# Softmax attention: the score maxima from the high halves alone, four heads at once on quarters of the array, in four banks, with one transpose of the maxima

## The reference

```python
q = x @ w_q + b_q                      # x is layernorm(x); 16 heads of 32 columns
k = context @ w_k + b_k
v = context @ w_v + b_v
scores = einsum('bqhd,bkhd->bhqk', q, k) * (1 / sqrt(32))
weights = softmax(scores, axis=-1)
out = einsum('bhqk,bkhd->bqhd', weights, v) @ w_o + b_o
```

## Time and profile before

| | us |
|---|---|
| median of 3 runs (1720.33 to 1724.28) | 1723.47 |
| the profiled execution | 1720.95 |
| its span | 1718.7 |
| softmax attention, first maximum to last output | about 648 to 1430 |
| one batch of it, in the middle | 94.35 |

### The profile page before, as it was taken

How to read it: one execution, slowest core, us unless ns; L and a number is a source line. 1 busy time by engine, 2 the same in 40 slices (tenths; PEclk the granted TensorE clock), 3 DMA queues, 4 the chain that set the end, 5 groups by cost and what they waited for, 6 DMA issues and landing times. The chain is left out here.

```text
span 1718.7 us, 29488 instructions
## 1 busy us (share of the span) xinstructions
PE 1586.6 (92%) x8932; PEld 719.5 (42%) x8932; DVE 1227.2 (71%) x1756; ACT 1138.3 (66%) x1895; POOL 1023.1 (60%) x738
## 2 busy tenths in 40 slices
PE   5999878998999977999999999999999988999998
PEld 3545433444444432334444444444444423444443
DVE  4978898997989745676676767676767766655553
ACT  5667599787888734665657666665657567556662
POOL 4777436666677723565657666675756665545452
PEclk9989999999999997999999999999999989999999
DMA  8410000000000112121211212121201110010001
GB/s 309 149 70 36 1 1 1 1 1 1 0 1 1 62 48 76 32 58 26 58 34 36 57 26 57 28 55 30 59 24 40 40 44 25 25 43 30 24 24 50
DMA packets 60463, 72.22 MB, mean 42 GB/s; under 512 B 14416, under 2 KB 40016, under 8 KB 59856
## 3 DMA queue, kind: packets, MB, share of 16 engines
q1 hardware_dynamic: 56944, 62.22, 12.3%
q10 hardware_dynamic: 3424, 8.91, 1.3%
HBM read 37.40 MB, written 8.39 MB: 27 GB/s over the span
## 5 line engine op out<-in xcount | busy, mean ns | idle before, releaser
L1556 DVE TENSOR_REDUCE s_mx<-bank 128x1 f32<-128x512 f32 x512 | 336.8, 684 | 198.5 <-PE bank L1684 192.5
L1443 ACT ACTIVATE s_E<-bank 128x512 f32<-128x512 f32 x512 | 293.7, 595 | 198.7 <-PE bank L1698 173.4
L1342 POOL TENSOR_TENSOR s_E<-s_E 128x1024 f32<-128x1024 f32 x128 | 300.5, 2367 | 122.0 <-PE bank L1706 114.5
L1684 PE MATMUL bank<-s_KA,s_QA 96*128 96x512 f16 x512 | 193.2, 388 | 17.3 <-DMA s_KA<-sm_cx 7.9
L1698 PE MATMUL bank<-s_QA,s_KA 97*128 97x512 f16 x512 | 195.7, 384 | 3.3 <-DMA s_QA<-s_mrow 1.1
L1335 POOL TENSOR_TENSOR sm_cx<-s_qkf,sm_cx 128x512 f16<-128x512 f32 x64 | 76.4, 1194 | 175.9 <-ACT sm_cx L1421 175.7
L1867 POOL TENSOR_TENSOR sm_cx<-m_xf,sm_cx 128x512 f16<-128x512 f32 x60 | 84.1, 1407 | 105.7 <-ACT sm_cx L1909 105.7
L1706 PE MATMUL bank<-s_E,s_V 128*32 128x512 f32 x1024 | 136.5, 605 | 4.3 <-ACT s_E L1443 4.3
L1075 PE MATMUL bank<-sm_zz,w1raw 128*128 128x512 f16 x256 | 99.4, 388 | 30.7 <-DVE sm_cx L962 15.5
L1098 PE MATMUL bank<-f_w2q,w2raw 128*128 128x512 f16 x512 | 121.8, 379 | 0.6 <-DVE w2raw L950 0.3
L772 POOL TENSOR_TENSOR sm_wkv<-sm_wkv,sm_cx 128x511 f32<-128x511 f32 x48 | 66.1, 1378 | 92.5 <-DVE sm_wkv L962 83.0
(11 more groups left out here) (264 smaller groups left out, 4078.6 us busy)
## 6 DMA issues: line engine op xcount, KB each, us to landing
sm_cx<-in_ctx SPq DMA_DIRECT2D x16, 768.0 KB, 4.5
s_QA<-sm_cx SPq DMA_DIRECT2D x384, 32.0 KB, 1.9
s_KA<-sm_cx SPq DMA_DIRECT2D x372, 32.0 KB, 1.9
X<-in_x SPq DMA_DIRECT2D x8, 1024.0 KB, 6.9
out_x<-X SPq DMA_DIRECT2D x8, 1024.0 KB, 4.3
w1raw<-in_w ACTq DMA_DIRECT2D x1, 4096.0 KB, 14.6
w2raw<-in_w ACTq DMA_DIRECT2D x1, 4096.0 KB, 28.2
w1raw<-in_wq SPq DMA_DIRECT2D x1, 1024.0 KB, 5.4
```

The source lines that it names most:

```text
L1342: e.tensor_tensor(into, into, other, ALU.add).then_inc(s_sum.sem, 1)
L1443: e.activation(E[:, SLOT[k] + h, :], SC[u % 2][:, :], ACT.Exp, scale=1.0 / float(np.sqrt(DH)))\
L1556: e.tensor_reduce(mx[:, q, h:h + 1], MX[q % 2][:, :], AX.X, ALU.max).then_inc(s_red.sem, 1)
L1684: e.matmul(MX[k % 2][:, :], QA[0:MROW, m, h, q * P:(q + 1) * P], KA[0:MROW, m, h, :], start=True, stop=True).then_inc(s_mx.sem, 1)
```

## The change

It does five things.

1. **Maxima from the high halves.** `maxima` multiplies the high half of the queries (32 rows of one head) by the high half of the keys, without stacking. Head h sits on partitions 32h to 32h + 31 of qkh, so four matmuls, one a head, use four row quarters of the array. Each writes a whole bank of its own: head h goes to bank h. A query tile of a group is one such **quad**; four quads a step instead of 16 full matmuls.
2. **The banks.** The quads write banks 0 to 3, that is, the two score banks too. The PSUM tensors become pairs of banks, so that one `tensor_reduce` reads two banks (128 x 2 x 512 to 128 x 2): two of them a quad, 8 a step instead of 16.
3. **Four phases a step.** At the start of each tile (u = 0, 4, 8, 12) TensorE waits for all exponentials so far, makes the quad for the next group, then the `attend` of the tile before (and at u = 0 and u = 8 one half of the denominators), and then waits for the first reduction (banks 0 and 1) before the tile's first score.
4. **One transpose.** mx is laid out so that a single transpose gives 16 x 128 in bank 2; mrow is 16 x 128, and the DMA spreads it. `rows` (transpose, copy and DMA) moves from the end of the step before to the start of the group's own step. The quad at u = 0 also waits for the copy (same bank).
5. **The rest of the order.** New tables; the work between two scores stands in `between(u)`. ScalarE's numerators and the division (`late`, now two steps after the group) move to the start of a step, ahead of the first exponential; `divided(b, 0)` to the end of step 2. GpSimd's second half of the sums moves to the start of the next step. qkh is double-buffered. Before the loop, the first group's maxima no longer wait for the stacking DMAs.

The diff, cut to what the prediction speaks of:

```diff
-        banks = [ctx.enter_context(nc.psum_tensor(f"bank{i}", [P, 512], F32)) for i in range(8)]
+        pairs = [ctx.enter_context(nc.psum_tensor(f"bank{i}", [P, 2, 512], F32)) for i in range(4)]
+        banks = [pairs[i // 2][:, i % 2, :] for i in range(8)]
...
+    Q_AT = ((-1, -1, 1, 3), (-1, -1, -1, -1), (0, 1, 2, 3), (-1, -1, 1, 3))
+    K_AT = ((3, 5, 7), (0, 1, 2), (7, 9, 11), (3, 5, 7))
+    V_AT = ((9, 11, 11, 13), (4, 6, 7, 7), (14, 15, 15, 15), (9, 11, 11, 13))
+    T_AT = (10, 12, 13, 15)
+    O_AT = ({}, {3: ((0, 0), (0, 1)), 5: ((0, 2),), 7: ((0, 3),), 8: ((1, 0),), 9: ((1, 1),), 11: ((1, 2), (1, 3)),
+                 13: ((2, 0),), 14: ((2, 1),), 15: ((2, 2), (2, 3))},
+            {5: ((3, 0),), 7: ((3, 1),), 11: ((3, 2),), 13: ((3, 3),)}, {})
+    RES_AT = ({}, {8: 0, 12: 1}, {-1: 2, 14: 3}, {})
+    STATS_AT, MOMENTS_AT, NORM_AT = {0: (0, 1), 4: (2, 3)}, 4, (0, 1, 2, 3)
...
-        SC, MX, NUM, DEN, R6, R7 = banks[0:2], banks[2:4], banks[4], banks[5], banks[6], banks[7]
+        SC, MX, MAXED, NUM, DEN, R6, R7 = banks[0:2], banks[0:4], pairs[0:2], banks[4], banks[5], banks[6], banks[7]
...
-        qkh, qkl = rows_of(cx, 4 * KC, 4 * KC + 2), rows_of(cx, 4 * KC + 2, 4 * KC + 4)
+        qkh = (rows_of(cx, 4 * KC, 4 * KC + 2), sb("qkh", [P, 2, S], F16))
...
@@ GpSimd, step @@
+                if m == 3:
+                    divided(b, 0)
+                if div:
+                    summed(*div, 1, 0)
+                    summed(*div, 1, 1)
+                if m == 2 and not last:
+                    context(b + 1)
+                if late and m != 2:
+                    divided(*late)
                 if proj:
-                    if m == 2:
-                        context(b + 1)
                     low(*proj, 0)
...
@@ ScalarE, rows and step @@
-                e.activation(mrow[:, :], MX[0][0:4, :], ACT.Copy, scale=-1.0 / MS).then_inc(s_mrow.sem, 1)
+                e.activation(mrow[:, :], MX[2][0:4 * TT, 0:P], ACT.Copy, scale=-1.0 / MS).then_inc(s_mrow.sem, 1)
-                e.dma_start(QA[MROW:MROW + 1, m, :, :], mrow[0:4, :]).then_inc(s_md[m].sem, 16)
+                e.dma_start(QA[MROW:MROW + 1, m, :, :].rearrange("o h (q n) -> o (h q) n", n=P), mrow[:, :]).then_inc(s_md[m].sem, 16)
...
+                rows(b, m)
+                if first and m == 0:
+                    e.wait_ge(s_lo, 2)
+                    e.wait_ge(s_raw[3], 32)
+                if div:
+                    numerators(*div)
+                if m == 1:
+                    queries(*proj, 0)
                 if m == 2 and not last:
                     for c in range(KC):
                         context(b + 1, c)
-                if proj:
-                    queries(*proj, 0)
-                if div and N_UNIT[m] < 0:
-                    numerators(*div)
+                if late and m != 2:
+                    divided(*late)
+                if m == 3 and not last:
+                    values(b + 1, 0)
                 for u in range(UNITS):
-                    if u == UNITS - 1 and nxt:
-                        rows(*nxt)
-                    if m == 1 and u - 1 in T_UNITS:
+                    exponential(b, m, u)
+                    if m == 1 and u in T_AT:
                         if last:
-                            shifted(T_UNITS.index(u - 1))
+                            shifted(T_AT.index(u))
                         else:
-                            high(b + 1, T_UNITS.index(u - 1), R7)
-                    exponential(b, m, u)
+                            high(b + 1, T_AT.index(u), R7)
                     if last and m == 3 and u in MIX_UNITS:
                         mix(MIX_UNITS.index(u))
-                    if div and u == N_UNIT[m]:
-                        numerators(*div)
-                    if proj and u == K_UNITS[m][-1] + 1:
+                    if proj and u == 3 and m != 1:
+                        queries(*proj, 0)
+                    if proj and u == (7, 3, 11, 7)[m]:
                         queries(*proj, 1)
-                    if proj and u == min(V_UNITS[m][-1] + 1, UNITS - 1):
+                    if proj and u == (13, 7, None, 13)[m]:
                         values(*proj)
-                    if m == 2 and u == A_LATE:
+                    if m == 2 and u == UNITS - 1:
                         divided(b, 0)
-                    if div and m != 1 and u == A_UNIT:
-                        divided(*div)
+                if last and m == 3:
+                    divided(b, 2)
...
@@ VectorE @@
-            def maximum(b, m, k):
-                h, q = divmod(k, TT)
+            def maxima(b, m, q):
                 s_mT.wait(e, b, m)
-                s_mx.wait(e, b, 16 * m + k + 1)
-                e.tensor_reduce(mx[:, q, h:h + 1], MX[q % 2][:, :], AX.X, ALU.max).then_inc(s_red.sem, 1)
+                s_mx.wait(e, b, TT * m + q + 1)
+                for i in range(2):
+                    e.tensor_reduce(mx[:, 2 * i:2 * i + 2, q], MAXED[i][:, :, :], AX.X, ALU.max).then_inc(s_red.sem, 1)
...
@@ TensorE @@
-            def maximum(b, m, k):
-                h, q = divmod(k, TT)
-                if k == 0:
-                    e.wait_ge(s_sh[m][0].sem, s_sh[m][0].count(b, NSH))
-                    e.wait_ge(s_sh[m][1].sem, s_sh[m][1].count(b, NSH))
+            def maxima(b, m, q):
+                if q == 0:
+                    e.wait_ge(s_qkh.sem, s_qkh.count(b, 2 * m + 2))
                     s_mrow.wait(e, b, m)
-                s_red.wait(e, b, 16 * m + k - 1)
-                e.matmul(MX[k % 2][:, :], QA[0:MROW, m, h, q * P:(q + 1) * P], KA[0:MROW, m, h, :],
-                         start=True, stop=True).then_inc(s_mx.sem, 1)
+                s_red.wait(e, b, 2 * (TT * m + q))
+                high = qkh[m % 2]
+                for h in range(4):
+                    head = slice(h * DH, (h + 1) * DH)
+                    last = e.matmul(MX[h][:, :], high[head, 0, q * P:(q + 1) * P], high[head, 1, :], start=True, stop=True)
+                last.then_inc(s_mx.sem, 1)
 
             def rows(b, m):
-                e.wait_ge(s_red.sem, s_red.count(b, 16 * (m + 1)))
-                for q in range(TT):
-                    last = e.transpose(MX[0][0:4, q * P:(q + 1) * P], mx[:, q, :], ident[:, :])
-                last.then_inc(s_mT.sem, 1)
-
-            def score(b, m, u):
+                e.wait_ge(s_red.sem, s_red.count(b, 2 * TT * (m + 1)))
+                e.transpose(MX[2][0:4 * TT, 0:P], mx[:, :, :].rearrange("p h q -> p (h q)"), ident[:, :]).then_inc(s_mT.sem, 1)
+
+            def score(b, m, u, nxt):
                 t, h = divmod(u, 4)
                 if u == 0:
+                    for w in range(2):
+                        e.wait_ge(s_sh[m][w].sem, s_sh[m][w].count(b, NSH))
                     e.wait_ge(s_md[m].sem, s_md[m].count(b, 1))
+                if nxt and h == 0:
+                    e.wait_ge(s_red.sem, s_red.count(nxt[0], 2 * (TT * nxt[1] + t) + 1))
...
+                def between(u):
+                    if m == 1 and u in T_AT:
+                        transposed(b + 1, T_AT.index(u), last)
+                    if proj:
+                        for c in range(KD):
+                            if Q_AT[m][c] == u and (u >= 0 or c):
+                                queries(*proj, 0, c)
+                        for c in range(KC):
+                            if K_AT[m][c] == u:
+                                queries(*proj, 1, c)
+                    if not first:
...
+                if proj and Q_AT[m][0] < 0:
+                    queries(*proj, 0, 0)
+                rows(b, m)
+                if first and m == 0:
+                    s_V.wait(e, 0, 2)
+                    e.wait_ge(s_lo, 2)
+                between(-1)
+                for u in range(UNITS):
+                    t, h = divmod(u, 4)
+                    if nxt and h == 0:
+                        if t == 0:
+                            s_mrow.wait(e, b, m + 1)
+                        e.wait_ge(s_ex.sem, s_ex.count(b, 16 * m + 4 * t))
+                        maxima(*nxt, t)
+                    if t and h == 0:
+                        attend(b, m, t - 1)
+                    if div and u == 0:
+                        attend(*div, TT - 1)
+                        denominators(*div, 0)
+                    if div and u == 4 * DN_TILE:
+                        denominators(*div, 1)
+                    score(b, m, u, nxt)
+                    between(u)
...
```

155 lines of the change are left out of this document (54 added, 101 removed).

## The result

| | before | after |
|---|---|---|
| median, 4 runs each on one chip | 1721.90 (1715.34 to 1724.28) | 1773.19 (1771.60 to 1775.68) |
| ratio, 95% interval | | 1.0306 (1.0277 to 1.0334) |
| span of the profiled execution | 1718.7 | 1773.8 |
| start of the channel mix, in the trace | 1431.77 | 1486.54 |

What follows compares the result with a forecast made beforehand. TensorE was taken as the bound before; its saving would lose to new waits, 101.5 against 94.35 us a batch. Seven batches (+ 50) less 7 before the loop gave 1764, median 1766 us; 8-in-10 range 1700 to 1805.

Steps and rivals of the forecast that it cites:

- likeliest case: The forecast itself: new waits make the softmax attention slower, 1766 us, own range 1740 to 1790, chance 0.60.
- TensorE's work: Per batch, falls from 93.8 to 84.6 us, quads at 0.39; pays only with new idle time under 9.8 us.
- The chain at a tile: Exponentials, quad, reduction (1.22) and score through shared banks: 2.42 us between tiles' exponentials, 4.67 a tile at least.
- The starts of the steps: From exponential 15 to the next first exponential: 4.4, 6.7 and 5.9 us for m = 0, 1, 3.
- The steps: The four steps of a batch take 21.9, 32.5, 23.7 and 23.4 us, sum 101.5 against 94.35.
- the named waits: Step 1: output chunk waits for a residual after both reductions, transpose for a low half behind reciprocals and division.
- The total: Seven full batches at 7.1 us more, 7 less before the loop: + 43 on the profiled 1720.95.
- Hidden: The later-issued DMA of maxima costs nothing: TensorE has 2.3 us of quad, attend and denominators between copy and first score.
- TensorE stays the bound: Rival: other work fills the waits, TensorE idles about 8 us a batch, 92.6 a batch, 1704 us; chance 0.21.
- The row quarters do not overlap: Rival: quad matmuls run one after another, + 0.64 on each of 16 chains, 72 us in all, 1838; chance 0.06.
- The clock falls: Rival: TensorE's clock drops after waits, 5 us a batch if a quarter of the groups' time ran at half, 1805; chance 0.08.
- That the two sides cancel: Rival: TensorE's saving and the new waits balance, 1720 to 1727 us; chance 0.05.

Runs made afterwards that it cites:

- half_reduce: The changed kernel with each maxima reduction over the first 256 of a bank's 512 columns: 1731.27 us, 1.0085 of the kernel before.
- one_row_quarter: The changed kernel with all four matmuls of a quad in head 0's row quarter, so they cannot overlap: 1852.30 us, 1.0796 of the kernel before.
- own_banks: The changed kernel's order, but maxima two heads at a time in banks 2 and 3 alone, outside the score banks: 1764.27 us, 1.0288 of the kernel before.
- half_and_late: The changed kernel with reductions over 256 of 512 columns and the late division moved behind exponential 3: 1727.92 us, 1.0067 of the kernel before.
- one_head: The kernel before with one transpose of maxima, and maxima from the high halves one head at a time: 1782.37 us, 1.0392 of the kernel before.

## Why the prediction was right, and where it was off

**The verdict and its mechanism** were right: 1773.19 against 1766, inside the likeliest case's own 1740 to 1790. The terms, in the order of the prediction:

**TensorE's work.** Forecast 84.6 us a batch, measured 87.75 busy. The quads cost what was put on them (16 x 0.33, and 0.09 more where no wait stands ahead, against 16 x 0.39). What the sum left out is next to them: each time TensorE stops, the last record's end counts as busy for 0.16 more (0.38 long, 0.22 held), at some 20 waits a batch, 3 us. So break-even lay at 6.6 us of idle time in the page's measure, not 9.8: half_reduce, with 8.8 us idle, is still the slower kernel. By the Trainium skill's 3.07x (TensorE: Matmul & The Clock Gate, Measured speedup vs the span model) a quad would be an estimated 0.28 us; here it is 0.24 without the change of form (0.33 less 0.09), 3.7 times as fast as four of 0.22.

**The chain at a tile.** Right in each link: 0.12 from exponentials to quad, 0.40, 0.12 to VectorE, a reduction of 1.22 (forecast 1.22, between bounds of 0.68 and 1.37), four exponentials in 2.21 to 2.25. The tiles of step 0 start their exponentials at 858.08, 863.20, 868.24 and 873.09, 15.0 us for three where the working gives 14.8. The Trainium skill's rule that packing does not speed up the emptying of PSUM (TensorEngine Tiling (Array Packing), PSUM Bottleneck) is what happened, with its limit: at a reduction of 0.69 it is no longer the bound, and the attend beside it is.

**The starts of the steps.** From the end of exponential 15 to the first exponential 4.1, 6.4 and 5.9 us for m = 0, 1 and 3, forecast 4.4, 6.7 and 5.9. The copy of the maxima was mis-sized: 0.25 to 0.27, as it has 128 columns, not the 0.59 of the 512-column one. That alone is the 0.3 of m = 0 and 1; for m = 3 it would make 5.6, so something there took 0.3 more than the working has.

**The steps.** Between copies 21.4, 32.5, 24.5 and 22.2 against 21.9, 32.5, 23.7 and 23.4: the sum 100.7 against 101.5. The prediction did not cut at the copies, though. Cut as it did, at the ends of exponential 15 and at the transpose between m = 1 and 2, the four are 21.6, 32.1, 23.5 and 23.5 us, each within 0.5. In step 1 the named waits are there, in TensorE's order of time:

```profile
887.00 0.39 PE L1709 MATMUL bank<-s_QA,s_KA 97*128 97x512 f16 x1 [0.48 <-DVE s_mx L1567]
...
894.81 0.39 PE L1655 MATMUL bank<-s_woh,s_ath 128*128 128x512 f16 x1 [0.95 <-DVE X L1581]
...
900.48 0.39 PE L1709 MATMUL bank<-s_QA,s_KA 97*128 97x512 f16 x1 [0.48 <-DVE s_mx L1567]
902.85 0.66 PE L151 MATMUL bank<-ident,s_z 128*128 128x128 f32 x4 [1.32 <-DVE sm_zz L1560]
905.92 0.66 PE L151 MATMUL bank<-ident,s_z 128*128 128x128 f32 x4 [0.69 <-DVE sm_zz L1560]
```

The output chunk waits for a residual behind both reductions, the last transpose for a low half behind the reciprocals and the division, as forecast. The longest wait, 1.32 at the transpose before it, is for a low half behind both reductions and a residual; the prediction does not name it. In step 2 exponential 14 waits for GpSimd's second sum by 1.13 (forecast 1.1), on ScalarE:

```profile
930.16 1.08 ACT L1451 ACTIVATE s_E<-bank 128x512 f32<-128x512 f32 x2 [1.13 <-POOL s_E L1343]
```

**The total.** Forecast 7 x 7.1 - 7 = 43, measured 55, and the agreement of the parts is not that of the sum. Ahead of the first copy the change gained 4.5 us (31.9 against 36.4 from the first matmul), not 7. The six middle batches lost 36.9, 6.2 each and not 7.1. The first and the last batch, which the prediction counted as one full batch together, lost 7.3 (99.24 against 91.98) and 17.4 (128.65 against 111.22, to the start of the channel mix), 24.7 in place of 7.1. Together that is 57.1, of which 2.4 us of scatter ahead of the softmax attention took back a part. That the total came within 12 us is in part luck: the middle was put too high and the two ends much too low. The last batch is the largest error. "Hidden" was wrong for the DMA there, and so was counting the last batch as any other:

```profile
1362.28 0.59 PE L1709 MATMUL bank<-s_QA,s_KA 97*128 97x512 f16 x2 [1.64 <-DMA s_QA<-s_mrow]
...
1436.48 0.59 PE L1709 MATMUL bank<-s_QA,s_KA 97*128 97x512 f16 x2 [1.44 <-DMA s_QA<-s_mrow]
...
1444.87 0.61 PE L1655 MATMUL bank<-s_woh,s_ath 128*128 128x512 f16 x1 [3.40 <-POOL s_atl L1348]
...
1458.99 1.93 PE L1717 MATMUL bank<-s_E,s_V 128*32 128x512 f32 x8 [1.71 <-ACT s_E L1451]
...
1473.02 1.94 PE L1725 MATMUL bank<-s_E,ones 128*32 128x512 f32 x8 [3.61 <-POOL s_E L1343]
```

Three of the last batch's four first scores wait for the DMA, 4.5 us in all (one does before, 1.15 us), and no score in any earlier batch of the changed kernel. In steps 0 and 2 the DMA itself took 3.9 and 3.7 us from issue to landing where the others took 1.65 to 2.4; next to the second a load of 1 MB for the channel mix is under way. In the last step it took 1.65, but the last group has no next maxima, and without a quad, which waits for the copy, attend and denominators run ahead of the copy and hide nothing. GpSimd's division low half and its second sums, moved to later places, now have nothing after them to hide behind (they held TensorE up for 0.47 and 0.62 before). After such waits attends take 1.93 us in place of 1.06 (one did before too), and over the last batch the mean granted clock is 0.89, where it was 0.94 before:

```profile
1357.89:1486.54 128.65, 95.41 (x555) 30.77 (x554) 71.82 (x80) 62.29 (x115) 69.13 (x43) 0.89 0.11 31
```

**The rivals.** *TensorE stays the bound* fell: it is 87% busy. *The row quarters do not overlap* fell; one_row_quarter gives its price, 79 us where 72 were forecast. *The clock falls* did not come in the middle (1.00), only in the last batch, where the kernel before has it too. (The 1.79 of those rows is a record, and is to be held against records of 1.04, not against the 0.88 from start to start.) *That the two sides cancel* fell with the first.

**What stays open.** own_banks has 8.3 us of idle time a batch, and half_reduce 8.8, although the shared banks are gone from the one and the long reduction from the other. In half_reduce the trace puts 3.2 us of it on scores that wait for the first exponentials of steps, 2.0 on the transposes of step 1 and 1.7 on quads that wait for the copy of the maxima. half_and_late took the first down to 0.2 and got 2.2 in step 1 for it; no run moved the others.

## What to carry to other kernels

A saving on the engine that is the bound counts only less what the new waits cost, so work out the break-even first (here 0.4 us of idle time a tile), and then look for the shortest cycle through a shared buffer: writer, reader, next writer. Packing small matmuls side by side pays by how many share one change of form; four a change halved the cost, two gave nothing, one lost. Work moved off a waited-for place must be followed on every engine that hands it on: the late division freed ScalarE in two steps and held up GpSimd in a third. And price the first and the last turn of a loop apart from the middle: what a reordering puts later is hidden only while something follows.

## What the runs showed of the hardware

A change between matmuls of 97 or 128 rows and matmuls of 32 rows in a row quarter costs TensorE 0.09 us each way (one_head: 0.31 to 0.32 from start to start, against 0.22), the same as between full and column-quarter matmuls. Two 32-row matmuls in one row quarter next to each other stand 0.22 apart like full ones. Four in four row quarters into four banks took 0.24 us besides the changes, two took 0.23. A reduction along the free dimension that spans two banks took 1.22 us for 1024 elements a partition, 0.69 for 512 and 0.42 for 256: 1.04 ns an element and 0.16 besides; 512 elements of one bank took 0.684 us, of two banks 0.689. ScalarE's copy of 16 x 128 took 0.25 to 0.27 us against 0.59 for 4 x 512, with 2048 elements in both, so it is the columns that cost here.
